# A transformer layer on one core: experts by sorted rows, placed between two attention heads

## The chip, the cores and the metric

The kernel runs on one core of a Trainium2 chip. Five engines work side by side and meet at semaphores: TensorE (PE in the profile, with its weight loads as PEld), VectorE (DVE), ScalarE (ACT), GpSimd (POOL) and SyncE (SP), which here only issues DMAs. ACT and POOL can issue DMAs too. The metric is the device time of one execution in microseconds; the number quoted is the median of three runs. One further execution was profiled, and all rows come from it.

## What is computed

The input x is 2 x 2048 rows of 256 numbers. Every row is normalised, and two branches read it: attention with 16 heads of width 16, and a gated expert layer in which each row uses only the expert with the largest of 8 logits. The experts' result goes through SiLU and multiplies the attention's.

```python
def experts(xf):                                   # xf: 4096 x 256
    logits = einsum('th,eh->te', xf, gate_w)       # 8 experts
    onehot = one_hot(argmax(logits, -1), 8)
    g = einsum('th,ehd->etd', xf, wg)              # wg, wu: 8 x 256 x 64
    u = einsum('th,ehd->etd', xf, wu)
    inter = square(relu(g)) * u * onehot.T[:, :, None]
    return einsum('etd,edh->th', inter, wd)        # wd: 8 x 64 x 256

xn = layernorm(x)
out = x + attention(xn, w_qkv, w_out) * silu(experts(xn))
```

Attention is softmax(q k / 4) v per head, with a rotation (RoPE) on q and k, and an output projection.

## The kernel before, in words

The 4096 rows are 32 tiles of 128. The kernel has three parts.

**The group part.** Eight groups of four tiles. For each tile PE multiplies the transposed rows by the weights of q, k, v and the gate (L757, L758). ACT copies the three results out of PSUM (L376 to L378), DVE rotates q and k (`rotate`, L494 to L501), PE transposes the rotated q and k (L790), ACT copies them as a high part (L385), DVE makes the low part that rounding lost (L528), and SP stores both with four DMAs to `parts_d` in DRAM (L265). Between these steps the group goes through all eight experts densely: `g` and `u` for four pairs of experts (L775, L781), a mask that PE makes of the one-hot choice (L798), DVE's and ACT's work on it (L522, L388, L537), the product with `wd` (L811), and SiLU into `gate` (L393). POOL normalises the next group's rows (L670, L676). PE transposes them (L729).

When the 16 tiles of batch 0 are stored, SP loads the q and k of head 0 back, stacked for two uses (`stack_loads`, L246 to L250): once for the row maxima ("a", partitions 64 up), once for the scores. From group 4 on, the maxima of head 0 are computed beside the group work (L742 on PE, L544 on DVE).

**The heads.** 32 heads (16 per batch), two per turn of a loop of 16 pairs. A head has 16 steps. In a step PE computes four blocks of scores (L838), four blocks for the maxima of a tile 21 steps ahead (L829), and the weighted values (L849); ACT takes the exponentials (L420); DVE reduces the maxima (L582). POOL copies a head's v into place before the head begins (L696, `stage`). SP loads later heads' q and k and stores sums.

**The end.** The output projection (L908), the product with `gate`, the sum with x, and the stores.

The order on each engine is written out by hand, each engine's program is a sequence of its own, and a wait is for a semaphore's count. The lines below are those of the functions that the change touches.

## Time and profile before

| what | us |
|---|---|
| median of 3 runs | 1772.77 (1771.05 to 1774.16) |
| the profiled execution | 1771.24 |
| its span, first to last instruction | 1769.4 |
| PE, DVE, ACT, POOL busy in the span | 1649.1, 1425.9, 1188.7, 56.9 |

The execution has 1.8 us around its span. A step in time is read by the number at the start of a row of the timeline, which is microseconds from the span's start. A group of instructions has the time for which they were busy, and behind it the time the engine stood idle ahead of them with what ended that.

### The profile page before, as it was taken

The page shows a single profiled execution, that of the slowest core. Times are in us where ns is not written, and L with a number is a line of the kernel's source. Part 1 is how long each engine was busy: PE and PEld are TensorE (multiplying, and loading weights), DVE is VectorE, ACT ScalarE, POOL GpSimd, SP SyncE. Part 2 cuts the span into 40 slices and gives each one's busy share as a digit, 9 for nine tenths or more (in the row PEclk, how much of TensorE's full clock was granted, in tenths as well). Part 3 has the DMA queues.
Part 4 walks back from the last instruction along what each step waited for, and adds up shares of the span by engine and source line. Part 5 has one row for each costly group of instructions (what it writes and reads, how often), then busy time and mean ns, then how long its engine had stood idle before and what let it go on. Part 6 is the DMA issues. An engine that isn't in the chain of part 4 may idle for free.

```text
span 1769.4 us, 30282 instructions
## 1 busy us (share of the span) xinstructions
PE 1649.1 (93%) x9536; PEld 717.0 (41%) x9536; DVE 1425.9 (81%) x1541; ACT 1188.7 (67%) x2314; POOL 56.9 (3%) x55
## 2 busy tenths in 40 slices
PE   5999999969999999999999999999999999999998
PEld 2555555433333333333333333333333333333335
DVE  6554666649999999999999999999999999999905
ACT  2333332228788777787777788777877778877781
POOL 1000000000000000000000100000010000000100
PEclk9999999969999999999999999999999999999999
DMA  4222211111111111211111113111111121111203
GB/s 159 65 66 67 77 48 48 49 60 30 43 42 42 42 39 39 70 56 39 39 39 40 43 43 90 44 45 43 42 41 42 61 69 41 39 39 39 58 4 111
DMA packets 71378, 92.66 MB, mean 52 GB/s; under 512 B 20273, under 2 KB 61361, under 8 KB 64177
## 3 DMA queue, kind: packets, MB, share of 16 engines
q1 hardware_dynamic: 65984, 85.23, 15.8%
q10 hardware_dynamic: 5360, 7.03, 1.1%
q8 instruction: 17, 0.28, 0.1%
q14 instruction: 17, 0.13, 0.0%
HBM read 66.01 MB, written 25.43 MB: 52 GB/s over the span
## 4 chain that ended last, share of the span: by engine, by line
PE 74%; ACT 16%; DVE 3%; issue 3%; DMA 3%; SPq 0%; DVEq 0%; ACTq 0%
PE ps L849 29%; PE ps L838 28%; ACT arena L420 16%; PE ps L781 3%; PE ps L811 3%; PE ps L757 3%; PE ps L775 2%; PE ps L758 1%; PE ps L829 1%; PE ps L742 1%; DMA x_sb<-in_x 1%; DVE arena L544 1%; PE ps L790 1%; DMA ks<-parts_d 1%; PE ps L908 1%
## 5 line engine op out<-in xcount | busy, mean ns | idle before, releaser
L582 DVE TENSOR_REDUCE arena<-ps 128x1 f32<-128x1024 f32 x992 | 1174.2, 1219 | 137.0 <-PE ps L829 131.3
L420 ACT ACTIVATE arena<-ps 128x512 f32<-128x512 f32 x2048 | 1059.8, 604 | 263.3 <-PE ps L838 261.8
L838 PE MATMUL ps<-qs,ks 50*128 50x512 f32 x2048 | 746.6, 444 | 62.0 <-ACT arena L420 30.3
L829 PE MATMUL ps<-ks,qs 48*128 48x512 f32 x1984 | 789.3, 470 | 12.8 <-DMA ks<-parts_d 11.8
L838 PEld LDWEIGHTS ps<-qs,ks 50*128 50x128 f32 x2048 | 338.3, 184 | 679.8 <-issue 429.1
L849 PE MATMUL ps<-arena 128*32 128x512 f32 x4096 | 546.2, 605 | 0.8 <-ACT arena L420 0.8
L829 PEld LDWEIGHTS ps<-ks,qs 48*128 48x128 f32 x1984 | 328.7, 185 | 55.1 <-DVE arena L582 13.5
L849 PEld LDWEIGHTS ps<-arena 128*32 128x32 f32 x4096 | 80.6, 108 | 128.8 <-ACT arena L420 114.3
L494 DVE TENSOR_TENSOR arena<-arena,rope 128x512 f32<-128x512 f32 x32 | 28.4, 887 | 86.6 <-ACT arena L378 85.7
L388 ACT ACTIVATE arena<-arena 128x512 f32<-128x512 f32 x32 | 20.1, 629 | 89.7 <-DVE arena L522 89.7
L757 PE MATMUL ps<-arena 128*128 128x512 f32 x128 | 69.4, 625 | 8.0 <-ACT arena L378 7.3
L811 PE MATMUL ps<-arena 128*128 128x256 f32 x256 | 60.7, 398 | 12.3 <-DVE arena L537 12.3
L775 PE MATMUL ps<-arena 128*128 128x512 f32 x128 | 62.6, 612 | 0.0
L781 PE MATMUL ps<-arena 128*128 128x512 f32 x128 | 60.2, 593 | 0.0
L811 PEld LDWEIGHTS ps<-arena 128*128 128x128 f32 x256 | 50.3, 199 | 21.4 <-DVE arena L537 8.1
L696 POOL COPY arena<-v_sb 128x256 f32 x32 | 13.2, 414 | 1267.2 <-ACT arena L412 1266.9
L614 DVE RECIPROCAL arena<-arena 128x16 f32<-128x16 f32 x33 | 8.0, 243 | 55.4 <-DMA arena<-arena 55.4
L376 ACT COPY arena<-ps 128x512 f32<-128x512 f32 x32 | 18.8, 587 | 48.1 <-PE ps L758 48.1
L544 DVE TENSOR_REDUCE arena<-ps 128x1 f32<-128x1024 f32 x32 | 39.1, 1221 | 3.6 <-PE ps L742 3.6
L758 PE MATMUL ps<-arena 128*128 128x264 f32 x128 | 40.4, 398 | 0.0
L758 PEld LDWEIGHTS ps<-arena 128*128 128x128 f32 x128 | 25.4, 198 | 32.9 <-issue 32.9
L393 ACT ACTIVATE gate<-ps 128x512 f32 (+1 forms) x16 | 9.6, 597 | 41.0 <-PE ps L811 40.9
(64 smaller groups left out, 571.0 us busy)
## 6 DMA issues: line engine op xcount, KB each, us to landing
parts_d<-arena SPq DMA_DIRECT2D x128, 128.0 KB, 2.0
qs<-parts_d SPq DMA_DIRECT2D x64, 256.0 KB
ks<-parts_d SPq DMA_DIRECT2D x64, 256.0 KB
qs<-parts_d SPq DMA_DIRECT2D x64, 128.0 KB
ks<-parts_d SPq DMA_DIRECT2D x64, 128.0 KB
onum_d<-arena SPq DMA_DIRECT2D x128, 32.0 KB, 1.9
out<-arena ACTq DMA_DIRECT2D x16, 256.0 KB, 2.4
arena<-onum_d SPq DMA_DIRECT2D x3, 1024.0 KB
```

The source lines that it names most:

```text
L420: nc.scalar.activation(prob[kb % 2][:, c * W:(c + 1) * W], ps[:, bank, :], ACT.Exp, scale=SCALE).then_inc(exp_done[bank], 1)
L494: nc.vector.tensor_tensor(ra.rearrange("p (h d) -> p h d", d=hd), q2, tab[:, :, 0:hd].to_broadcast([P, 2 * QK // DH, hd]), ALU.mult)
L544: nc.vector.tensor_reduce(most[0][:, t, u:u + 1], ps[:, 6:8, :], AX.XY, ALU.max).then_inc(a_reduced[u], 1)
L582: nc.vector.tensor_reduce(most[head_slot][:, tile, u:u + 1], ps[:, AB + 2 * u:AB + 2 + 2 * u, :], AX.XY, ALU.max).then_inc(a_reduced[u], 1)
L757: nc.tensor.matmul(ps[:, o, :], xt, w_sb[:, k, 0:QK], start=(k == 0), stop=(k == KC - 1))
L758: last = nc.tensor.matmul(ps[:, o + 1, 0:VG], xt, w_sb[:, k, QK:QK + VG], start=(k == 0), stop=(k == KC - 1))
L775: last = nc.tensor.matmul(ps[:, o, :], wg_sb[:, k, c * P:(c + 1) * P], xnT[s][:, k, :], start=(k == 0), stop=(k == KC - 1))
L781: last = nc.tensor.matmul(ps[:, o + 1, :], wu_sb[:, k, c * P:(c + 1) * P], xnT[s][:, k, :], start=(k == 0), stop=(k == KC - 1))
L811: last = nc.tensor.matmul(ps[:, 6 + j // 2, (j % 2) * D:(j % 2 + 1) * D], inter[:, c, j * P:(j + 1) * P], wd_sb[:, c, :], start=(c == 0), ...
L829: ins = nc.tensor.matmul(ps[:, AB + c, :], qs[head_slot][ABASE:ABASE + KR, tile * P:(tile + 1) * P].bitcast(F32R), ks[head_slot][ABASE:ABA ...
L838: nc.tensor.matmul(ps[:, bank, :], ks[s][0:KS, kb * P:(kb + 1) * P].bitcast(F32R), qs[s][0:KS, c * W:(c + 1) * W].bitcast(F32R), start=Tru ...
L849: last = nc.tensor.matmul(ps[32 * c:32 * (c + 1), PVB, :], vst[s][:, kb, :], prob[kb % 2][:, c * W:(c + 1) * W], start=(kb == 0), stop=(kb ...
```

## The change

The dense experts leave the group part. In their place:

- **Group part.** The four-tile groups become a stream of tiles: PE makes q, k, v and logits of tile t, and transposes q and k of tile t - 2. The normalised rows go into `gate`, which is free until the experts write it. ACT first issues 13 DMAs that zero a sorted copy of the rows in DRAM (`xs_d`). From tile 20 (`EARLY`) on the maxima of head 0 run beside it, as before from group 4 on. When batch 0 is stored, SP now loads the stacks of heads 0 and 1 together.
- **Routing.** After the last tile DVE finds each row's expert, POOL counts rows per expert by a running sum, PE adds the counts over partitions, and DVE turns them into offsets. Each expert's rows are padded to whole tiles of 128, at most 39 tiles in all (`NF`). DVE also writes the expert of each of the 39 tiles.
- **Scatter and gather.** POOL writes the 4096 rows to their sorted places with 32 indirect DMAs of 128 rows (`place`, while heads 0 and 1 run), and collects the results with 32 more (`collect`, from head 4 on).
- **The experts' stage.** After two pairs of heads (`FB`), all engines leave the heads and go through 39 tiles. The expert's number is read from SBUF into a register of PE, and the weights are addressed by it.

```diff
-                for c in range(EC):
-                    for k in range(KC):
-                        last = nc.tensor.matmul(ps[:, o, :], wg_sb[:, k, c * P:(c + 1) * P], xnT[s][:, k, :],
+                for i in range(NF + 2):
+                    if i < NF:
+                        which[i] = pe.value_load(expert[0:1, i:i + 1], min_val=0, max_val=E - 1)
+                        pe.wait_ge(xs_out, i + 1)
+                        if i:
+                            pe.wait_ge(relu_done, i)
+                            pe.wait_ge(hu_ready, i)
+                        for k in range(KC):
+                            last = nc.tensor.matmul(ps[:, AB + 1, 0:2 * DE], xsT[i % 2][:, k, :],
+                                                    wgu[:, k, bass.ds(which[i], 1), :], start=(k == 0), stop=(k == KC - 1))
+                        last.then_inc(hid_done, 1)
+                    if i + 1 < NF:
+                        turn_sorted(i + 1)
+                    if 1 <= i <= NF:
+                        pe.wait_ge(inter_ready, i)
+                        if i >= 2:
+                            pe.wait_ge(inter_out, i - 1)
+                        nc.tensor.transpose(ps[:, AB + 2, 0:P], inter[(i - 1) % 2], ident[:]).then_inc(inter_turned, 1)
+                    if i >= 2:
+                        pe.wait_ge(inter_out, i - 1)
+                        if i >= 3:
+                            pe.wait_ge(y_out, i - 2)
+                        nc.tensor.matmul(ps[:, AB + 3, 0:D], interT[(i - 2) % 2], wd2[:, bass.ds(which.pop(i - 2), 1), :],
+                                         start=True, stop=True).then_inc(y_done, 1)
...
-            with pe.Fori(0, NP - 1) as pi:
+            with pe.Fori(0, FB) as pi:
+                pair(pi, False)
+            experts()
+            with pe.Fori(FB, NP - 1) as pi:
                 pair(pi, False)
...
+            def load_sorted(i):
+
+                if i >= XR:
+                    sp.wait_ge(xs_turned, i - XR + 1)
+                sp.dma_start(xs[i % XR], xs_d[i * P:(i + 1) * P, :]).then_inc(xs_loaded[i % XR], 16)
...
+            def experts():
+
+                for i in range(NF + 2):
+                    if i + 2 < NF and i + 2 >= XR:
+                        load_sorted(i + 2)
+                    if i >= 2:
+                        store_sorted(i - 2)
...
                 if b == 0:
+                    for i in range(2):
+                        sp.wait_ge(parts_stored[i], PSTORES * NB2)
                     sp.wait_ge(first_ones, 2)
                     stack_loads(sp, 0, qs[0], ks[0], ABASE, a_loaded[0])
                     stack_loads(sp, 0, qs[0], ks[0], 0, loaded[0])
-            sp.wait_ge(u_done, NT)
+                    stack_loads(sp, 1, qs[1], ks[1], ABASE, a_loaded[1])
+                    stack_loads(sp, 1, qs[1], ks[1], 0, loaded[1])
...
+                for t in range(NT):
+                    nc.gpsimd.indirect_dma_start(xs_d, bass.IndirectOffsetOnAxis(ap=pos[:, t:t + 1], axis=0),
+                                                 gate[:, t, :], None).then_inc(rows_sorted, 16)
```

`turn_sorted` waits for a tile's load (four buffers, `XR`), and transposes its two halves. In the stage ACT copies the transposed rows, takes the relu of g and the SiLU of y; DVE forms relu(g) * u * relu(g) and copies its transpose. `store_sorted` waits for the SiLU (`y_out`) and stores the tile.

**On PE, in the group part.** Before, in a group's second half (L757 and L758 are the fourth tile's last products, L775 and L781 the dense experts', L790 transposes, L798 masks):

```order
L757 MATMUL ps<-arena 128x512
L758 MATMUL ps<-arena 128x264
L771 REGISTER_ALU
L775 MATMUL ps<-arena 128x512 x2
L790 MATMUL ps<-ident,arena 128x128 x4
L781 MATMUL ps<-arena 128x512 x2
L794 REGISTER_ALU
L798 MATMUL ps<-ident_b,arena 64x128 x8
```

After, one tile from tile 20 on (L935 and L936 are q, k, v and logits, L958 the early maxima, L921 the next rows' transposes, L946 those of q and k):

```order
L935 MATMUL ps<-arena 128x512
L936 MATMUL ps<-arena 128x264
L958 MATMUL ps<-ks,qs 128x512 x2
L921 MATMUL ps<-ident,gate 128x128 x4
L946 MATMUL ps<-ident,arena 128x128 x4
L958 MATMUL ps<-ks,qs 128x512 x2
```

The experts' products and masks are gone from between the tiles, and the transposes of a tile's q and k come after the products of the tile two later.

**On SP, between the stores of batch 0 and of batch 1.** Before, the eight loads of head 0's two stacks:

```order
L265 DMA parts_d<-arena 128x2x128 x64
L246 DMA qs<-parts_d 32x1x2048
L248 DMA qs<-parts_d 16x2048
L249 DMA ks<-parts_d 32x1x2048
L250 DMA ks<-parts_d 16x2048
L246 DMA qs<-parts_d 32x1x2048
L248 DMA qs<-parts_d 16x2048
L249 DMA ks<-parts_d 32x1x2048
L250 DMA ks<-parts_d 16x2048
L265 DMA parts_d<-arena 128x2x128 x64
```

After, the end of the sixteen, ahead of the stores of batch 1 (L289 to L293 are the same four loads):

```order
L289 DMA qs<-parts_d 32x1x2048
L291 DMA qs<-parts_d 16x2048
L292 DMA ks<-parts_d 32x1x2048
L293 DMA ks<-parts_d 16x2048
L308 DMA parts_d<-arena 128x2x128 x64
```

Eight loads more stand on this queue ahead of the stores of tile 16 and up.

**On PE, between the second and the third pair of heads.** Before there is only the loop's turn. After, one tile of the stage (L1054 turns the rows of the next tile, L1068 reads the expert's number into a register, L1074 is g and u, L1083 turns the product, L1088 is y of the tile two back):

```order
L1068 TENSOR_LOAD arena
L1068 ISA x2
L1074 ISA
L1074 MATMUL ps<-arena 128x128
L1074 ISA
L1074 MATMUL ps<-arena 128x128
L1054 MATMUL ps<-ident,arena 128x128 x2
L1083 MATMUL ps<-ident,arena 128x128
L1088 ISA
L1088 MATMUL ps<-arena 128x256
```

39 such pieces stand between head 3 and head 4, with no work of the heads among them.

## Rows read from the trace of the kernel before

**Rows 1.** Page, part 2: PE's busy share in tenths, 40 slices.

```profile
PE   5999999969999999999999999999999999999998
```

**Rows 2.** Windows: busy us (and instructions) of PE, PEld, DVE, ACT, POOL; clock; DMA.

```profile
80.00:120.00 40.00, 38.73 (x166) 22.18 (x164) 21.75 (x38) 13.75 (x29) 4.17 (x2) 1.00 0.20 53
...
520.00:560.00 40.00, 38.12 (x248) 15.07 (x245) 36.55 (x36) 31.60 (x61) 0.41 (x1) 1.00 0.12 39
```

**Rows 3.** Timeline of PE over one group: start, duration, engine, line, shapes.

```profile
103.68 1.02 PE L757 MATMUL ps<-arena 128*128 128x512 f32 x2
...
114.13 1.88 PE L775 MATMUL ps<-arena 128*128 128x512 f32 x4
...
132.43 1.09 PE L729 MATMUL ps<-ident,arena 128*128 128x128 f32 x8
...
134.79 7.17 PE L811 MATMUL ps<-arena 128*128 128x256 f32 x32 [1.27 <-DVE arena L537]
...
141.80 1.02 PE L757 MATMUL ps<-arena 128*128 128x512 f32 x2
```

**Rows 4.** Timeline: ACT's first copies after the products of a tile.

```profile
31.14 0.58 ACT L376 COPY arena<-ps 128x512 f32<-128x512 f32 x1
...
31.88 0.19 ACT L378 COPY arena<-ps 128x8 f32<-128x8 f32 x1
```

**Rows 5.** Timeline: DVE's rotation of one tile, the low part behind it.

```profile
122.56 0.68 DVE L494 TENSOR_TENSOR arena<-arena,rope 128x512 f32<-128x512 f32 x1
...
124.56 0.68 DVE L528 TENSOR_TENSOR arena<-ps,arena 128x512 fp32r<-128x512 f32 x1
125.16 0.68 DVE L522 TENSOR_TENSOR arena<-arena,ps 128x512 f32<-128x512 f32 x1
```

**Rows 6.** Timeline: the same rotation while POOL normalises rows.

```profile
111.46 2.28 POOL L670 TENSOR_TENSOR arena<-x_sb,mean 128x1024 f32 x1 [34.52 <-DVE arena L501]
...
111.91 2.12 DVE L496 TENSOR_TENSOR arena<-arena,rope 128x256 f32<-128x256 f32 x1
...
113.94 2.13 DVE L498 TENSOR_TENSOR arena<-arena,rope 128x256 f32<-128x256 f32 x1
```

**Rows 7.** Groups by line, 0 to 375 us: busy, mean ns, idle before, releaser.

```profile
L544 DVE TENSOR_REDUCE arena<-ps 128x1 f32<-128x1024 f32 x32 | 39.1, 1221 | 3.6 <-PE ps L742 3.6
...
L377 ACT COPY v_sb<-ps 128x256 f32 (+1 forms) x32 | 12.2, 380 | 0.0
```

**Rows 8.** Timeline of the SP queue: 16 stores, then loads of stacks, and PE.

```profile
120.59 13.23 SPq L265 DMA_DIRECT2D parts_d<-arena  x16
...
355.81 0.65 SPq L246 DMA_DIRECT2D qs<-parts_d  x1
...
362.91 5.46 SPq L248 DMA_DIRECT2D qs<-parts_d  x1
...
369.08 4.70 SPq L250 DMA_DIRECT2D ks<-parts_d  x1
372.92 1.35 PEld L829 LDWEIGHTS ps<-ks,qs 48*128 48x128 f32 x4 [12.15 <-DMA ks<-parts_d]
```

**Rows 9.** Windows while stacks load: the last two numbers are DMA share and GB/s.

```profile
190.00:192.00 2.00, 2.00 (x6) 0.68 (x4) 1.97 (x3) 1.21 (x4) 0.95 (x1) 1.00 0.13 53
```

**Rows 10.** DMA issues: queue, count, KB each, median us from issue to landing.

```profile
parts_d<-arena SPq DMA_DIRECT2D x128, 128.0 KB, 2.0
...
ident<-in_ident ACTq DMA_DIRECT2D x1, 64.0 KB, 3.0
```

**Rows 11.** Timeline: maxima ahead of head 0, and the first exponentials.

```profile
376.71 2.36 DVE L582 TENSOR_REDUCE arena<-ps 128x1 f32<-128x1024 f32 x2 [0.18 <-PE ps L829]
...
379.24 2.36 DVE L582 TENSOR_REDUCE arena<-ps 128x1 f32<-128x1024 f32 x2 [0.18 <-PE ps L829]
...
386.81 3.60 ACT L420 ACTIVATE arena<-ps 128x512 f32<-128x512 f32 x7
```

**Rows 12.** Windows ahead of head 0: the number behind the brackets is the granted clock.

```profile
378.00:380.00 2.00, 2.00 (x4) 0.97 (x4) 1.82 (x2) 0.00 (x0) 0.00 (x0) 0.50 0.13 53
```

More of the change, by code:

```diff
@@ L334, in pair @@
                         load_a(n + 3, 1 - s)
+                    if between and s:
+                        between()
                     store_sums(n, s, pi)
@@ L426, in _ @@
             exps(0, 1, False)
-            with act.Fori(1, NP) as pi:
+            for pi in range(1, FB):
+                for s in range(2):
+                    exps(pi, s, False)
+            experts()
+            with act.Fori(FB, NP) as pi:
                 for s in range(2):
@@ L577, in _ @@
+            for t in range(NT - LAG, NT):
+                low_part(t)
             nc.vector.memset(spread[1], 1.0)
@@ L604, in _ @@
+            choose()
+            for t in range(NT - EARLY, KB):
+                for u in range(2):
+                    reduce(t, 0, t, u)
+            base[0], count[0] = SETUP_STEPS + NT, 0
             for k in range(CUTS):
@@ L679, in group, with step @@
-            def group(n, s, has_next):
-                if has_next:
-                    pool.wait_ge(rope_done, past(n * GT + 1))
-                    center(n + 1, 1 - s)
-                    scale(n + 1, 1 - s)
-            with pool.Fori(0, NG // 2 - 1) as gp:
-                for s in range(2):
-                    group(gp * 2 + s, s, True)
-            group(NG - 2, 0, True)
-            group(NG - 1, 1, False)
+            def step(ins):
+                done[0] += 1
+                ins.then_inc(pool_step, 1)
+                pool.wait_ge(pool_step, done[0])
@@ L817, in _ @@
[L817 to L822 removed]
+            turn_x(0, 0)
+            turn_x(0, 1)
+            for t in range(NT):
+                n, j = divmod(t, GT)
+                qkv(t)
+                if t >= EARLY:
+                    score_early(t - EARLY, 0)
+                if j < 2 and n + 1 < NG:
+                    turn_x(n + 1, j)
+                if t >= LAG:
+                    turn_q(t - LAG)
+                if t >= EARLY:
+                    score_early(t - EARLY, 1)
@@ L824, in score_a @@
+            for t in range(NT - LAG, NT):
+                turn_q(t)
             def score_a(t, head_slot, tile, c):
```

624 lines of the change are left out of this document (373 added, 251 removed).

## The prediction, made before the result was known

> **What bounds the kernel now.** I read the slices first: PE is at nine tenths nearly throughout [rows 1]. Then two windows of 40 us. In the group part PE works 38.7 of 40 us while DVE has 21.8; in the heads PE has 38.1 and DVE 36.6 [rows 2]. So PE sets both, the group part alone has other engines with room, and nothing can be hidden under the heads if it needs PE. The timeline of a group says what PE does in 38.1 us (103.68 to 141.80): 10.4 us of q, k, v and logits, 18.3 us in which the dense experts alternate with the transposes of q and k, 2.4 us of row transposes and a wait, 7.0 us of the products with wd [rows 3]. All but some 13 us of it is the experts'. The first exponential of head 0 stands at 386.8 us [rows 11]; from there to the end the change leaves the program as it is, but for a stage put between heads 3 and 4. The sum is therefore: how much earlier head 0 begins, less what the stage takes.
>
> **Group part, tiles 0 to 19.** A tile's products are 10.4 / 4 = 2.6 us of PE. With the experts gone, what is late next? I follow the loop: products of tile t 2.6, ACT's three copies 0.9 (31.14 to 32.07) [rows 4], DVE's rotation 2.0 and the low part of tile t - 2 0.6 [rows 5], four transposes on PE 0.55 (half of eight in 1.09 [rows 3]), and then the products of tile t + 2, which stand behind these in PE's order. That is 6.7 us, with five hand-offs of 0.1 us 7.2 us, for two tiles: 3.6 each. DVE alone would take 2.6, SP's four stores 13.23 / 4 = 3.3 [rows 8]. POOL's two normalising operations per group make two operations of DVE last 2.1 us in place of 0.4: 3.4 us per four tiles [rows 6]. Fully on the path this makes 4.45, fully absorbed 3.6; I take 4.2, near the upper end, since DVE has only 1 us of slack a tile. ACT's 13 zeroing DMAs stand ahead of its first copy, about 0.45 us each, some 6 us; the experts' weights are no longer loaded beside x, which gives back about 5 us. I leave the first copy at 31.1 us (28 to 37). The low part of tile 15 is ready 17 tiles later: 31.1 + 17 x 4.2 + 3.5 = 106.
>
> **The sixteen loads.** Here I expect the largest loss. A load of 256 KB with an outer dimension of two keeps two of sixteen DMA engines busy (share 0.13) and moves 53 GB/s [rows 9]: 4.9 us. Sixteen loads hold eight of them: 39.6 us on the same two engines. SP itself is held up: in the trace the tenth load of a series waits 5.5 us for room and the twelfth 4.7 us [rows 8]. The stores of tile 16 stand behind, on the same queue and partly the same engines. ACT waits for their landing before it copies the high part of tile 18, and PE, DVE and ACT stop one after the other. From the ready tile 15: stores 3.3, landing 2.0 [rows 10], loads 39.6, stores landing about 3: 48 us, so work goes on at 154. Undisturbed it would have been there at about 119, so the stall is 35 us. Its lower bound is the wait for the first stack alone, which took 17 us from issue in the trace (355.81 to 372.92 [rows 8]): 106 + 5 + 17 = 128, a stall of 9. Its upper bound adds a quarter to the loads: 45.
>
> **Tiles 20 to 31.** DVE now has 2 x 1.22 of maxima [rows 7] with 2.6: 5.1 us, and a hand-off through PE: 5.3. From 154: 2 for what is left of tile 20, 11 x 5.3 = 58, 4 for POOL's last group, 4 for the last two tiles' transposes: 222.
>
> **Up to head 0.** DVE's routing comes first, seven operations, about 2.5 us. Then the maxima of tiles 12 to 20 of the count, nine at 2.53 us (376.71 to 379.24 [rows 11]), 22.8 us, where the kernel before has five left. The counts and PE's first scores are 4 more, and 2 for DVE's twelve operations on the offsets, which stand ahead of the heads' reduces: 253. Before: 386.8. POOL's running sum, about ten small operations, lies under the 22.8 us; without that cover it would cost 5 us. **Gain 134 us**, between 115 (longer tiles and stall) and 160 (short stall).
>
> **The stage.** Nothing of it is in the trace, so I bound a tile from both sides. Below: g and u four passes of 128 columns, 0.43 plus 0.17 to drain, relu 0.2, the copy of the next rows 0.38 [rows 7], hand-offs: 1.5 us. The loop through memory is longer: SP stores tile i - 2 only when its SiLU is done, and issues the load of a later tile behind that store. Turning the loaded rows 0.27, the product's transpose 0.14, y 0.6, SiLU 0.38, store and load issue 0.8, landing 2.0 to 3.0 [rows 10], hand-offs 0.4: 4.6 to 5.6 us for two tiles, 2.3 to 2.8 each. The register load stands between the tiles on PE with no row of its own; it is bounded by 0.1 and by a DMA's way to memory, 2.0 [rows 10]. In the middle it hides in the loop above. If all is in series at half clock, 2.4 us of PE and 2.0 of load: 4.4. I take 2.5: 39 x 2.5 = 98. Entry is 3 us, two last rounds 3, the way back 6 (a table load of ACT, refilling of PE's pipeline, a slow clock): **cost 110 us**, between 70 and 184.
>
> The Trainium skill's "Runtime: NRT & Kernel Launch", section "Instruction fetch mechanics", gives about 0.2 us for a register's load, from HBM, and 1.3 us for several; no run here shows one from SBUF. By 1.3 us the stage stays at 110.
>
> **POOL.** 32 scatters must be issued between the start of head 0 plus 8 us and the start of head 2, since the staging of v for heads 2 and 3 stands behind them; a head is 16 steps of 2.6 us, so 84 - 8 = 76 us, or 2.4 us each. The gathers have 82 us before head 6. The nearest rows are SP's and ACT's issues, 0.35 to 0.85 us, and POOL's own operation of 2.3 us [rows 6, 8]. I take 1.5 us, hidden, cost nothing. If the cover is gone, each us beyond 2.4 costs 32 us, and again in the gathers.
>
> **Sum:** 1771.2 - 134 + 110 = **1747 us** for the profiled execution; the runs' median lies 1.5 us above it, less than I can tell.
>
> **Rivals.**
> 1. *The stage crawls: slower than before.* The break-even is a tile of (134 - 12) / 39 = 3.1 us. The place is PE's order: the register load waits until y is issued, and the next g and u wait for the load. 
> 2. *The loads do not block, and the stage flows.* Stall 10 us, tile 2.2: gain 159, cost 98: 1710. For it: the group part of before did not visibly stop at its eight loads. Against: it had 17 us between them and the next store. Chance 0.2.
> 3. *POOL is late.* An indirect DMA of 3.3 us: 29 us ahead of head 2 and about 24 ahead of head 6: 1800. Nothing in the trace excludes it. Chance 0.1.
> 4. *The change does not do what it says:* the group part stays as long since DVE and SP, not PE, set it. By 3.6 to 4.45 us a tile against 9.5 before this is excluded for the first 20 tiles; it survives only as the stall, which is in the sum.
>
> **How the numbers follow.** My forecast has 0.52, and its own range is 1715 to 1772 (gain 120 to 150, cost 90 to 125, not both at their worst). The whole range leaves out 0.1 at either end: 1695 to 1805. A measurement of this kernel can tell about 0.2%, 3.5 us, from no change. Faster than 1769: rival 2 and nearly all of the forecast's range, 0.70. Within: 0.06. Slower: rivals 1 and 3, less their lower ends, 0.24.
>
> **What would show it.** Head 0's first exponential near 253 us (rival 2: 228). The high part of tile 18 idle ahead for some 35 us, released by a landing of `parts_d`. Tiles 3.6 to 4.45 us apart before, 5.3 after. In the stage, starts of g and u 2.5 us apart (3.6 in rival 1, the wait ending at the register load or at PE), and granted clock. PE's wait for v's staging at heads 2 and 6 zero (rival 3: tens of us). Heads otherwise at 2.6 us a step. I am wrong if the scatter slows the heads' own steps, or if the code, now written out in place of loops, makes engines wait for instructions: nothing here prices either.

## The result

| | before | after |
|---|---|---|
| median, us | 1773.47 (1771.05 to 1774.26, 4 runs) | 1848.97 (1842.84 to 1860.97, 4 runs) |
| span of the profiled execution | 1769.4 | 1848.8 |
| first exponential of head 0 | 386.8 [rows 11] | 282.9 |
| from there to the end | 1382.6 | 1565.9 |

The ratio after to before is 1.0443, 95% interval 1.0418 to 1.0468: 4.4% slower, outside the forecast range. Below, "the rest" is the time from head 0's first exponential to the end of the span. The group part gave back 103.9 us (134 were forecast), and the rest grew by 183.3 us (110 were forecast).

The slices first: page of after, part 2, PE and POOL, 46.2 us each, against [rows 1].

```profile
PE   4763875899877499999999999999999999999998
...
POOL 1120106000002400000000100000001000000100
```

PE now has three holes. The fourth slice is the stacks' loads. The seventh (scatter) and the fourteenth (gather) are where POOL has 6 and 4 tenths of its own. The stage, mostly in the eleventh to thirteenth, has 8, 7 and 7 tenths.

ACT copies a head's sums once (L519, `sums_out`). Two such copies are one head apart, which gives a ruler for the second part. Timeline of ACT in after: start and duration of these copies.

```profile
364.37 0.59 ACT L519 COPY arena<-ps 128x512 f32<-128x512 f32 x1 [0.15 <-PE ps L1004]
406.50 0.59 ACT L519 COPY arena<-ps 128x512 f32<-128x512 f32 x1 [0.18 <-PE ps L1004]
448.33 0.59 ACT L519 COPY arena<-ps 128x512 f32<-128x512 f32 x1
583.89 0.60 ACT L519 COPY arena<-ps 128x512 f32<-128x512 f32 x1
665.88 0.59 ACT L519 COPY arena<-ps 128x512 f32<-128x512 f32 x1 [0.23 <-PE ps L1004]
```

A head without disturbance takes 42 us (364.37 to 406.50, 406.50 to 448.33). Head 0, with the scatter, takes 81.5 us from its first exponential. Head 4, with the gather, takes 82.0 (583.89 to 665.88). What happens in head 4 is in the timeline of all engines: the number in brackets is the idle time ahead of the instruction.

```profile
599.27 0.95 POOL L867 DMA_INDIRECT gate<-ys_d,arena  x1 [0.30 <-issue]
...
602.02 0.60 ACT L527 ACTIVATE arena<-ps 128x512 f32<-128x512 f32 x1 [2.91 <-issue]
602.66 0.28 PEld L993 LDWEIGHTS ps<-qs,ks 50*128 50x128 f32 x1 [2.41 <-issue]
602.66 0.79 PE L993 MATMUL ps<-qs,ks 50*128 50x512 f32 x1 [1.69 <-issue]
...
623.10 0.95 POOL L867 DMA_INDIRECT gate<-ys_d,arena  x1 [0.30 <-issue]
623.72 0.60 ACT L527 ACTIVATE arena<-ps 128x512 f32<-128x512 f32 x1 [21.11 <-remote]
...
624.37 0.79 PE L993 MATMUL ps<-qs,ks 50*128 50x512 f32 x1 [18.88 <-issue]
...
629.32 1.23 DVE L642 TENSOR_REDUCE arena<-ps 128x1 f32<-128x1024 f32 x1 [24.68 <-remote]
```

POOL issues one gather every 1.25 us, from 585 to 625 us. From 604.7 to 623.7 no other engine does anything but finish one product. The profile names no releaser for these waits: "issue" is none that it shows, "remote" is a semaphore event whose source it does not know. The program has none of the three wait for POOL there, except for v, which was staged before the first gather. Counted one to one, product by product, the exponential at 623.72 reads the scores that PE finished at 603.45 (602.66 + 0.79), 20 us earlier. So what is late is the hand-off from one engine to the next, not an engine's own work; how it comes to be late the profile does not show. The windows show the same, against 38.12 of 40 us before [rows 2] (busy us and instructions of PE, PEld, DVE, ACT, POOL; granted clock; DMA share; GB/s):

```profile
280.00:320.00 40.00, 21.67 (x92) 8.15 (x91) 17.23 (x26) 13.64 (x25) 27.24 (x32) 0.63 0.24 87
480.00:560.00 80.00, 60.40 (x340) 38.67 (x336) 30.65 (x103) 37.52 (x105) 0.00 (x0) 0.98 0.34 103
600.00:640.00 40.00, 15.40 (x51) 5.19 (x53) 8.54 (x8) 6.92 (x14) 19.21 (x21) 0.50 0.26 77
```

The DMA engines are at a quarter in these windows (at 0.37 in 605 to 623 us alone), so they are not what is full. TensorE's granted clock falls to 0.50, its 1.2 GHz, in the hole. In the stage it is 0.98.

The group part, in the order of time (timelines of ACT's queue, ACT and PE):

```profile
26.77 11.22 ACTq L478 DMA_DIRECT2D xs_d<-arena  x13
38.03 0.59 ACT L461 COPY arena<-ps 128x512 f32<-128x512 f32 x1 [11.04 <-PE ps L936]
...
96.64 0.66 PE L921 MATMUL ps<-ident,gate 128*128 128x128 f32 x4 [3.93 <-POOL gate L827]
...
123.22 0.68 DVE L617 TENSOR_TENSOR arena<-ps,arena 128x512 fp32r<-128x512 f32 x1
...
144.19 1.22 PE L958 MATMUL ps<-ks,qs 48*128 48x512 f32 x2 [13.42 <-DMA ks<-parts_d]
...
178.79 0.59 ACT L469 CAST arena<-ps 128x512 fp32r<-128x512 f32 x1 [31.72 <-DMA parts_d<-arena]
```

The thirteen zeroing DMAs keep ACT from its first copy for 11.2 us, 0.86 us each. PE waits at the first tile of a group for the rows that POOL normalises. The low part of tile 15 is made at 123.2. The first stack makes PE wait 13.4 us ahead of the first maxima (L958). The sixteen loads stop ACT for 31.7 us ahead of the high part of tile 18, released by a landing of `parts_d`, as the forecast had it.

### The profile page after: what moved, and what is told of

Its sections match the earlier page's. It is cut to its first block, busy times and chain, and to the rows that moved or that the text cites. A ratio compares the mean times of both kernels' runs of the same rounds, so it can differ in the third digit from the quotient of the medians.

```text
span 1848.8 us, 29654 instructions
## 1 busy us (share of the span) xinstructions
PE 1598.4 (86%) x9121; PEld 681.0 (37%) x9121; DVE 1395.5 (75%) x1573; ACT 1191.3 (64%) x2361; POOL 128.9 (7%) x142
## 4 chain that ended last, share of the span: by engine, by line
PE 63%; ACT 17%; DMA 5%; issue 5%; DVE 4%; another core or an unknown queue 3%; SPq 2%; POOL 1%; ACTq 1%; DVEq 0%; POOLq 0%
PE ps L1004 27%; PE ps L993 27%; ACT arena L527 15%; DMA arena<-xs_d 3%; PE ps L935 2%; PE ps L984 2%; PE ps L936 1%; DVE arena L642 1%; DMA x_sb<-in_x 1%; DMA parts_d<-arena 1%; PE ps L1118 1%; PE ps L958 1%; PE ps L1074 1%; PE ps L1088 1%
## 5 line engine op out<-in xcount | busy, mean ns | idle before, releaser
L993 PE MATMUL ps<-qs,ks 50*128 50x512 f32 x2048 | 767.8, 453 | 110.9 <-ACT arena L527 45.7
L984 PE MATMUL ps<-ks,qs 48*128 48x512 f32 x2000 | 816.3, 480 | 11.7 <-issue 6.3
L874 POOL COPY arena<-v_sb 128x256 f32 (+1 forms) x32 | 13.9, 436 | 1337.6 <-ACT arena L519 1298.3
L935 PE MATMUL ps<-arena 128*128 128x512 f32 x128 | 83.6, 741 | 0.7 <-ACT arena L452 0.7
L461 ACT COPY arena<-ps 128x512 f32<-128x512 f32 x32 | 18.8, 589 | 96.7 <-PE ps L936 96.7
L946 PE MATMUL ps<-ident,arena 128*128 128x128 f32 x128 | 23.2, 311 | 33.4 <-DVE arena L617 33.4
L921 PE MATMUL ps<-ident,gate 128*128 128x128 f32 x64 | 13.1, 340 | 42.4 <-POOL gate L827 25.2
L469 ACT CAST arena<-ps 128x512 fp32r<-128x512 f32 x32 | 19.0, 593 | 44.2 <-DMA parts_d<-arena 32.4
L617 DVE TENSOR_TENSOR arena<-ps,arena 128x512 fp32r<-128x512 f32 x32 | 21.9, 683 | 33.4 <-ACT arena L469 33.4
L936 PE MATMUL ps<-arena 128*128 128x264 f32 x128 | 45.1, 438 | 0.0
L936 PEld LDWEIGHTS ps<-arena 128*128 128x128 f32 x128 | 29.1, 227 | 41.0 <-issue 41.0
L1074 PE MATMUL ps<-arena 128*128 x156 | 28.8, 310 | 9.5 <-issue 7.7
```

The costliest lines, as they stand in the source:

```text
L617: nc.vector.tensor_tensor(lo, ps[:, 5, :].rearrange("p (m t) -> p m t", m=HM), pst[t % 2][:, 0:HM, :], ALU.subtract).then_inc(pt_out, 1)
L935: nc.tensor.matmul(ps[:, o, :], xt, w_sb[:, k, 0:QK], start=(k == 0), stop=(k == KC - 1))
L936: last = nc.tensor.matmul(ps[:, o + 1, 0:VG], xt, w_sb[:, k, QK:QK + VG], start=(k == 0), stop=(k == KC - 1))
L946: last = nc.tensor.transpose(ps[:, 5, q * P:(q + 1) * P], rq[t % 2][:, q * P:(q + 1) * P], ident[:])
L984: ins = nc.tensor.matmul(ps[:, AB + c, :], qs[head_slot][ABASE:ABASE + KR, tile * P:(tile + 1) * P].bitcast(F32R), ks[head_slot][ABASE:ABA ...
L993: nc.tensor.matmul(ps[:, bank, :], ks[s][0:KS, kb * P:(kb + 1) * P].bitcast(F32R), qs[s][0:KS, c * W:(c + 1) * W].bitcast(F32R), start=Tru ...
```

## The experiments

Thirteen kernels and the kernel after. Their main numbers, all in us: the time of the run, head 0's first exponential, the rest, head 0 (with the scatter), and the heads in which the gathers are issued.

| kernel | time | first exp. | rest | head 0 | gather's heads |
|---|---|---|---|---|---|
| after | 1848.97 | 282.9 | 1565.9 | 81.5 | 82.0 |
| e1_later_turn | 1852.48 | 281.9 | 1569.0 | 79.9 | 84.9 |
| e2_one_per_step | 1776.06 | 276.9 | 1497.2 | 44.3 | 45.1 + 47.6 |
| e3_plain_dmas | 1765.93 | 276.9 | 1487.3 | 44.5 | 46.4 |
| e4_no_indirect | 1770.21 | 279.5 | 1489.0 | 44.1 | none: 44.9, 43.0 |
| e5_bursts | 1813.59 | 277.6 | 1533.9 | 45.4 | 55.2 + 59.7 + 53.3 |
| e6_plain_pool | 1771.59 | 280.1 | 1489.8 | 44.3 | 43.4 |
| e7_quarter_bytes | 1851.16 | 285.8 | 1563.6 | 78.8 | 80.8 |
| g1_spread_loads | 1746.74 | 250.4 | 1494.3 | 47.2 | 43.6 + 46.2 |
| g2_table_once | 1732.67 | 250.4 | 1480.2 | 44.6 | 44.6 + 44.0 |
| h2_fixed_expert | 1733.12 | 249.8 | 1481.2 | 44.1 | 46.5 + 49.0 |
| g3_group_part | 1724.94 | 237.1 | 1485.8 | 44.3 | 44.6 + 47.5 |
| g4_gather_slower | 1716.75 | 235.8 | 1480.7 | 44.5 | 43.6, 43.1, 41.9, 42.4 |
| n1_own_pause | 1737.65 | 249.8 | 1486.1 | 44.5 | 46.5 + 47.2 |

All but after and g4 are single executions, and the four of after lie up to 18 us apart. The first exponential of kernels with the same group part differs by up to 6 us from one to the next, so the parts are compared, not the totals.

### Is it the indirect DMAs, and what about them?

**e4_no_indirect.** Both loops of `indirect_dma_start` are left out.

```diff
-                for t in range(NT):
-                    nc.gpsimd.indirect_dma_start(xs_d, bass.IndirectOffsetOnAxis(ap=pos[:, t:t + 1], axis=0),
-                                                 gate[:, t, :], None).then_inc(rows_sorted, 16)
...
-                for t in range(NT):
-                    nc.gpsimd.indirect_dma_start(gate[:, t, :], None, ys_d,
-                                                 bass.IndirectOffsetOnAxis(ap=pos[:, t:t + 1], axis=0)).then_inc(gate_ready, 16)
```

> Neither scatter nor gather is issued: the experts work on the zeroed copy, and the product at the end takes the normalised rows in place of the experts' result. The rest of the program is that of after. Theories A and B: the time of a head returns to that of before (first head 42 to 45 us instead of 82) and the kernel takes 1849 - 37.5 - 52 = 1760 us, plus or minus 6. Theory C (code): the holes stay, 1849.

The sums' copies, timeline of ACT:

```profile
323.63 0.59 ACT L519 COPY arena<-ps 128x512 f32<-128x512 f32 x1 [0.15 <-PE ps L997]
...
541.27 0.60 ACT L519 COPY arena<-ps 128x512 f32<-128x512 f32 x1
586.21 0.59 ACT L519 COPY arena<-ps 128x512 f32<-128x512 f32 x1 [0.23 <-PE ps L997]
```

Head 0 takes 44.1 us and head 4 takes 44.9: the scatter costs 37.3 us and the gather 37.1. The rest is 1489.0 against 1565.9, so the indirect DMAs cost **76.9 us**. I had put 52 us on the gather in the expectation, by reading one long idle as a loss; the ruler of copies says 37, and the kernel came at 1770.21, above the 1760 plus or minus 6 that I expected. The rest is still 106.4 us above that of before: this is the stage, with the table loads behind it (g2 below).

**e1_later_turn.** The gathers are issued after v is staged for heads 6 and 7, in the second turn of the loop.

```diff
-            collect()
             for s in range(2):
                 stage(0, FB + 1, s, FB + 1)
+            collect()
```

> The same kernel as after, but the 32 gathers are issued one pair of heads later, in the second turn of the loop that follows the stage; everything is still computed. In the kernel after, head 4 and 5 lose about 52 us while POOL issues the gathers, and PE's long idle is put down to 'issue'. Theory A (each indirect DMA that POOL prepares holds up the hand-offs of the other engines while it is prepared): the hole of some 50 us moves to heads 6 and 7, the time stays at 1849 us, plus or minus 8. Theory B (the hole comes from moving the 4 MB): the same as A, 1849. Theory C (the engines run out of code, since the gathers fall into the first turn of a loop, whose code isn't there yet): no hole at heads 6 and 7 and none at heads 4 and 5, about 1797 us.

Timeline of ACT:

```profile
668.82 0.61 ACT L519 COPY arena<-ps 128x512 f32<-128x512 f32 x1
715.75 2.08 ACT L527 ACTIVATE arena<-ps 128x512 f32<-128x512 f32 x4 [20.42 <-remote]
753.74 0.59 ACT L519 COPY arena<-ps 128x512 f32<-128x512 f32 x1 [0.23 <-PE ps L1004]
```

The hole moves with the gathers: the head from 668.82 takes 84.9 us, and ACT stands for 20.4. The theory of missing code, which "issue" suggested, has fallen.

**e7_quarter_bytes.** Rows of 64 numbers to and from an array of their own, zeroed by four more DMAs.

```diff
-                    nc.gpsimd.indirect_dma_start(xs_d, bass.IndirectOffsetOnAxis(ap=pos[:, t:t + 1], axis=0),
-                                                 gate[:, t, :], None).then_inc(rows_sorted, 16)
+                    nc.gpsimd.indirect_dma_start(few_d, bass.IndirectOffsetOnAxis(ap=pos[:, t:t + 1], axis=0),
+                                                 gate[:, t, 0:64], None).then_inc(rows_sorted, 16)
```

> The 32 scatters and 32 gathers are indirect as in the kernel after and follow on each other without a pause, but each row has 64 numbers (256 bytes) and goes to and comes from an array of its own, so a quarter of the bytes moves and the experts work on the zeroed copy. Four more zeroing DMAs stand in ACT's queue at the start, some 3 us. Theory A/A2 (the preparing, which goes by the number of rows): pitch 1.27 us and the same two losses, 38 and 52 us, plus or minus 10: 1850. Theory B (the moving of bytes): losses of a quarter, some 22 us together, 1783.

Waits of the whole kernel, us in total, times, longest:

```profile
ACT arena L531 <- remote: 66.0, 12, 22.5
DVE arena L646 <- remote: 64.2, 5, 20.5
```

Heads of 78.8 and 80.8 us with a quarter of the bytes. Moving the data is not the cause.

**e3_plain_dmas** and **e6_plain_pool.** In e3 the scatters are 32 plain DMAs of POOL, the gathers 32 plain ones of SP. In e6 both are 64 plain DMAs of half a tile, issued by POOL.

```diff
+                    nc.gpsimd.dma_start(xs_d[t * P:(t + 1) * P, :], gate[:, t, :]).then_inc(rows_sorted, 16)
...
+                sp.dma_start(gate[:, t, :], ys_d[t * P:(t + 1) * P, :]).then_inc(gate_ready, 16)
```

```diff
+                    for h in range(2):
+                        nc.gpsimd.dma_start(xs_d[t * P:(t + 1) * P, h * P:(h + 1) * P],
+                                            gate[:, t, h * P:(h + 1) * P]).then_inc(rows_sorted, 16)
```

> The rows are not sorted here, so the experts work on the wrong rows, with the same number of tiles and bytes: the 32 scatters become 32 plain DMAs of 128 KB issued by POOL, and the 32 gathers become 32 plain DMAs of 128 KB issued by SP after the stage. Theory A (preparing on POOL): the gather's 52 us are gone, since POOL prepares nothing there; the scatter's 37 us shrink if a plain DMA is prepared faster than 1.27 us, and stay if not: 1760 to 1797 us. Theory B (moving 4 MB in rows of 1 KB beside the heads): both losses stay, 1849. Theory C: both stay, 1849.

> The rows are not sorted and not collected by index, so the experts work on the wrong rows; tiles and bytes are the same. In place of 32 indirect DMAs POOL issues 64 plain DMAs of half a tile (128 rows of 512 bytes) in each of the two places, without a pause; at the 0.54 us each that the run with 32 plain ones shows, this is 34 us of uninterrupted issue, nearly the 40 us of the indirect ones. Theory P (any DMA that POOL prepares does it, and the 17 us of the earlier run were too short for it to build up): a standstill in both places, 20 to 50 us each, 1800 to 1850. Theory I (only the indirect form does it): no standstill, 1760 to 1770 us.

POOL's timeline in e6:

```profile
284.93 34.08 POOL L859 DMA_DIRECT2D xs_d<-gate  x64 [0.72 <-POOL arena L854]
...
544.70 34.31 POOL L869 DMA_DIRECT2D gate<-ys_d  x64 [0.19 <-issue]
```

POOL issues without a pause for 34 us, 0.53 us each, and heads 0 and 4 take 44.3 and 43.4 us: no loss. The same bytes, by plain DMAs of 128 rows each, disturb nobody. It is the indirect form, or what only it does here, which is to go to scattered rows: an indirect DMA to rows that lie in order was not run, so the two are not told apart. e3 agrees for the scatter (44.5); its gather's head took 46.4, 1.5 us more than in e4.

### How often may they be issued?

**e2_one_per_step.** POOL waits for one step of the heads before each.

```diff
                 for t in range(NT):
+                    pool.wait_ge(a_scored[1], AHEAD + 1 + t)
                     nc.gpsimd.indirect_dma_start(xs_d, bass.IndirectOffsetOnAxis(ap=pos[:, t:t + 1], axis=0),
                                                  gate[:, t, :], None).then_inc(rows_sorted, 16)
+                    if t == KB + 4:
+                        stage(0, 1, 0, 1)
```

> Everything is computed, but POOL waits for a step of the heads before each of the 32 scatters and each of the 32 gathers, so that one is issued every 2.6 us in place of every 1.27 us. Theory A with a fixed price for each indirect DMA (1.2 us in the scatter, 1.6 us in the gather): the loss is spread but stays, 1849 us plus or minus 10. Theory A2 (what holds up the others is that POOL issues them without a pause, the delay builds up over some 8 to 20 us and then everything stands): with a pause behind each, nearly all of the 90 us come back, 1760 to 1775 us. Theory B (data): 4 MB over twice the time, at most half of the loss stays, 1800. Theory C (code): nothing changes, 1849.

The rest falls from 1565.9 to 1497.2, 8.2 above the kernel without any: 69 of the 77 us come back with the same 64 DMAs. The theory of a fixed price per DMA has fallen. The kernel's 1776.06 is 1 us above the range expected of the theory that holds.

**e5_bursts.** Bursts of 4 per 4 steps in the scatter, of 8 per 8 steps in the gather.

```diff
+                    if t % 4 == 0:
+                        pool.wait_ge(a_scored[1], AHEAD + 4 + t)
...
+                    if t % 8 == 0:
+                        pool.wait_ge(a_scored[1], FB * 2 * KB + AHEAD + 8 + t)
```

> Everything is computed. The scatters are issued in bursts of 4, one burst every 4 steps of the heads, and the gathers in bursts of 8, one burst every 8 steps; within a burst nothing is waited for. A burst of 4 is about 5 us of POOL, one of 8 about 10 us. In the kernel after, the first idle time of the other engines comes some 5 to 12 us behind the first DMA, the standstill 11 to 19 us behind it. Theory A2 (the delay builds up while they are issued without a pause, and is gone with a pause): bursts of 4 cost under 3 us over both heads together, bursts of 8 cost between 0 and 15 us; the whole kernel 1770 to 1790 us. Theory A (a price per DMA, which the spacing of the run with one per step hid for another reason): each burst stops the others for its length, 1849.

The first burst of 8 (timelines of POOL, ACT and DVE):

```profile
571.63 1.01 POOL L873 DMA_INDIRECT gate<-ys_d,arena  x1 [24.10 <-PE ps L990]
...
580.46 0.95 POOL L873 DMA_INDIRECT gate<-ys_d,arena  x1 [0.30 <-issue]
...
580.29 1.09 ACT L527 ACTIVATE arena<-ps 128x512 f32<-128x512 f32 x2 [3.39 <-remote]
...
582.41 2.36 DVE L642 TENSOR_REDUCE arena<-ps 128x1 f32<-128x1024 f32 x2 [4.95 <-remote]
```

The bursts of 4 cost 1.3, 3.0 and 1.6 us in three heads, 6 together. The bursts of 8 cost 10.3, 16.6 and 11.3, 38 together: as much as 32 without a pause. My expectation was wrong in all three numbers: at most 15 us for the bursts of 8, under 3 us for those of 4, and 1770 to 1790 us for the kernel. The first idle time comes after the fourth or fifth DMA, 5 to 6 us after the first of the burst.

**n1_own_pause.** On g2 (below), without waits for steps: POOL clears a small array twice behind each scatter and once behind each gather.

```diff
-                    pool.wait_ge(a_scored[1], AHEAD + 1 + t)
                     nc.gpsimd.indirect_dma_start(xs_d, bass.IndirectOffsetOnAxis(ap=pos[:, t:t + 1], axis=0),
                                                  gate[:, t, :], None).then_inc(rows_sorted, 16)
+                    for _ in range(2):
+                        step(nc.gpsimd.memset(held[0], 0.0))
```

> The run with the table loaded once, but POOL waits for no step of the heads: behind each scatter it clears a small unused array twice, behind each gather once, each clearing about 0.45 us and waited for, so that the pitch is about 2.2 us in the scatter and 1.75 us in the gather, against 1.27 in the kernel after and 2.6 with one per step. Everything is computed. Theory D (what counts is the share of POOL's time that goes to preparing indirect DMAs; the other engines' hand-offs are late only while that share is nearly one, or builds up when it is over some bound): nearly no loss in the scatter (first head 44 to 46 us), less than half of the 37 us loss in the gather; the kernel 1733 to 1755 us. Rival E (it was the meeting with the heads' steps that helped, which keeps each DMA away from the hand-offs): both losses back in full, about 37 us each, 1805 us. Rival F (POOL being busy without a pause, with whatever work): both losses back or larger.

POOL's timeline in the gather:

```profile
515.37 0.96 POOL L875 DMA_INDIRECT gate<-ys_d,arena  x1 [0.27 <-POOL arena L877]
516.32 0.44 POOL L877 MEMSET arena<- 128x384 f32 x1
517.03 0.95 POOL L875 DMA_INDIRECT gate<-ys_d,arena  x1 [0.27 <-POOL arena L877]
```

POOL is as busy as ever, and the holes are gone. At a pitch of 2.15 us head 0 takes 44.5 us (0.4 lost), at 1.66 us the gather's two heads 93.7 us against 88.0 in e4 (5.7 lost), at 1.25 one head loses 37. So 0.4 us more between two indirect DMAs takes most of the loss away, whoever makes the pause. The gathers that are paced by steps, 2.6 us apart, lose 0.5 to 7.5 us in their two heads (e2, g1, g2, h2, g3), so these single runs do not tell 1.66 from 2.6 us.

### The group part, the stage, and the loop behind it

**g1_spread_loads.** On e2: after batch 0 only the first four loads, the other twelve one per tile.

```diff
                     stack_loads(sp, 0, qs[0], ks[0], ABASE, a_loaded[0])
-                    stack_loads(sp, 0, qs[0], ks[0], 0, loaded[0])
-                    stack_loads(sp, 1, qs[1], ks[1], ABASE, a_loaded[1])
-                    stack_loads(sp, 1, qs[1], ks[1], 0, loaded[1])
...
+                    if b and 2 <= t < 14:
+                        head, base, done = ((1, ABASE, a_loaded[1]), (0, 0, loaded[0]), (1, 0, loaded[1]))[(t - 2) // 4]
+                        stack_loads(sp, head, qs[head], ks[head], base, done, ((t - 2) % 4,))
```

> The run with one indirect DMA per step, with one edit in the group part: after batch 0 only the four loads of head 0's first stack are issued, and the other twelve follow one at a time behind the stores of tiles 18 to 29. Everything is computed. My theory of the stall (sixteen loads hold two DMA engines for some 40 us and the stores behind them wait): the stall of 30 us ahead of the high part of tile 18 shrinks to under 12 us, the first exponential comes at 277 - 22 = 255 us and the kernel takes 1754 us, plus or minus 8. Rival (the loads only delay what DVE and PE would be late with anyway, or each single load holds up the stores of its tile by 5 us): first exponential 270 to 277, kernel 1769 to 1776.

Timeline of PE:

```profile
140.75 1.22 PE L966 MATMUL ps<-ks,qs 48*128 48x512 f32 x2 [11.18 <-DMA ks<-parts_d]
```

The stall of 31.7 us is gone; what stays is the wait for the first stack, 11.2 us (13.4 in after). The first exponential comes at 250.4, 26.5 us earlier.

**g2_table_once.** While comparing e4 with before I found that a pair of heads takes 85.0 us behind the stage and 84.2 before. The cause is in e4's timeline of ACT and DVE, once per turn of the loop:

```profile
1136.43 1.28 ACT L527 ACT_TABLE_LOAD   x1
...
1139.43 1.23 DVE L642 TENSOR_REDUCE arena<-ps 128x1 f32<-128x1024 f32 x1 [0.94 <-PE ps L977]
```

and in the groups of after and of g2 (busy us, mean ns):

```profile
L527 ACT ACT_TABLE_LOAD x15 | 19.2, 1283 | 1.2 <-PE ps L993 0.9
```

```profile
L531 ACT ACT_TABLE_LOAD x2 | 2.6, 1283 | 0.9 <-PE ps L1003 0.9
```

The loop is entered with SiLU's table, so the exponential's load stands inside it and runs in each of 14 turns. The Trainium skill's "ScalarE: Activation LUTs", section "What ACT_TABLE_LOAD costs", gives about 1283 ns for a load; the trace agrees, 1283 ns. g2 writes the first pair behind the stage out:

```diff
+            for s in range(2):
+                exps(FB, s, False)
-            with act.Fori(FB, NP) as pi:
+            with act.Fori(FB + 1, NP) as pi:
```

> The run with spread loads, with one edit: ACT's exponentials of heads 4 and 5 are written out ahead of its loop, so that the loop is entered with the exponential's table in place. In the kernel after, ACT's L527 has 15 table loads of 1.28 us, one at the entry and one in each of the loop's 14 turns, and a pair of heads takes 85.0 us there against 84.2 before. Theory (the load stands inside the loop because SiLU was the table ahead of it, and 0.8 of its 1.28 us are not hidden): 2 loads are left (one ahead of head 0, one ahead of head 4), a pair takes 84.2 us again, the kernel 1746.7 - 11 = 1736 us, plus or minus 3. Rival (the 0.8 us are the loop's turn or its code): loads gone, time 1745 to 1748.

A pair takes 84.2 us again (1021.75 to 1105.97), and the rest is 14.1 us shorter than in g1. From the end of head 5 on the two kernels differ by 9.9 us: these are the loads of the 13 turns behind it, 0.76 us each. The other 4.2 lie before, mostly in heads 0 and 5, whose length differs by 2 to 3 us among runs with the same pacing; with them the kernel came out just below the expected 1733 to 1739.

**h2_fixed_expert.** On g2; the experts' numbers are constants, so no register is read.

```diff
-                        which[i] = pe.value_load(expert[0:1, i:i + 1], min_val=0, max_val=E - 1)
+                        which[i] = i % E
```

> The run with the table loaded once, but the expert of a tile is a constant and no register is read on PE, so the rows go through the wrong experts; everything else is the same. Theory (the stage's loop is the one through memory and the queue, the register's load hides beside it): the stage's 39 tiles take the same time within 5 us, kernel 1731 to 1737. Rival (the load stands in series on PE): 39 times 0.6 to 1.0 us come back, kernel 1697 to 1713.

The copies around the stage, first in h2, then in g2 (timelines of ACT):

```profile
377.85 0.58 ACT L523 COPY arena<-ps 128x512 f32<-128x512 f32 x1 [0.15 <-PE ps L1014]
...
507.15 0.61 ACT L523 COPY arena<-ps 128x512 f32<-128x512 f32 x1
```

```profile
379.16 0.59 ACT L523 COPY arena<-ps 128x512 f32<-128x512 f32 x1
...
512.22 0.60 ACT L523 COPY arena<-ps 128x512 f32<-128x512 f32 x1
```

129.3 against 133.1 us, 3.8 less. But over the same stretch the kernels whose stage is unchanged lie between 130.9 (e3) and 137.2 us (e2), so one execution of each only bounds the price of the 39 register loads, at 0.2 us each or less. How the price is hidden shows in PE's groups of the stage, first g2, then h2 (idle time behind the second bar):

```profile
L1084 PE MATMUL ps<-arena 128*128 x156 | 28.8, 310 | 9.5 <-issue 7.5 <-ACT arena L499 1.5
L1064 PE MATMUL ps<-ident,arena 128*128 128x128 f32 x78 | 16.9, 300 | 10.4 <-DMA arena<-xs_d 9.6 <-DVE arena L648 0.5
```

```profile
L1084 PE MATMUL ps<-arena 128*128 128x128 f32 x156 | 28.1, 304 | 1.3 <-ACT arena L499 1.3
L1064 PE MATMUL ps<-ident,arena 128*128 128x128 f32 x78 | 17.2, 303 | 19.4 <-DMA arena<-xs_d 18.8 <-DVE arena L648 0.5
```

Without the loads PE's idle time ahead of g and u (L1084) falls from 9.5 to 1.3 us, 0.2 us a tile, and its wait for the rows from memory (L1064) grows from 9.6 to 18.8. The tile stays bound by the loop through memory. The total is the same since the two heads of the gather took 7.0 us more in h2 than in g2, within the spread of this paced gather in the other kernels.

**g3_group_part.** On g2: the zeroing DMAs one per tile from tile 3 on, POOL's normalising two tiles earlier.

```diff
+                if 3 <= t < 3 + NF // ZR:
+                    zero_rows(t - 3)
...
-                    pool.wait_ge(rope_done, (n - 1) * GT)
+                    pool.wait_ge(rope_done, (n - 1) * GT - 2)
```

> The run before with two edits in the group part, seen at different places of the trace: ACT issues the 13 zeroing DMAs one per tile from tile 3 on, not ahead of its first copy, and POOL normalises a group's rows two tiles earlier. Theory: the first copy of a tile comes at 27 to 28 us in place of 38 (11 us), and the tile period falls from 5.0 to 4.2 us since PE no longer waits for POOL at a group's first tile (7 groups, 3 to 5 us each in the first five): first exponential 250 - 11 - 16 = 223 us, kernel 1709 us, plus or minus 8. Rival (POOL's two operations slow DVE wherever they lie, and 0.86 us of issue in each tile is paid there): first exponential 238, kernel 1725.

Timeline of PE in the first tile:

```profile
31.42 1.11 PE L934 MATMUL ps<-ident,gate 128*128 128x128 f32 x4 [9.52 <-POOL gate L836]
```

13.3 us of the 27 expected. ACT's first copy came 11 us earlier, but PE then waited for POOL's first group until 31.4, which the zeroing had covered. The period of a tile fell from 4.97 to 4.42 us (from POOL's second start to its sixth, 16 tiles), not to 4.2. PE's waits for POOL at the later groups, 3.5 to 3.9 us in g2, are gone. So the theory did not hold in full: the recorded rival, that POOL's two operations slow DVE wherever they lie and that the zeroing DMAs' issue is paid in each tile, named 238 us and 1725, and 237.1 and 1724.94 came. Its two parts were not taken apart.

**g4_gather_slower.** On g3: one gather per two steps, with v of the later heads staged in between.

```diff
-                    pool.wait_ge(a_scored[1], FB * 2 * KB + AHEAD + 1 + t)
+                    pool.wait_ge(a_scored[1], FB * 2 * KB + AHEAD + 1 + 2 * t)
```

> The run with both edits of the group part, with the gathers one per two steps of the heads in place of one per step, so over four heads; everything is computed. With one per step the second head of the gather takes 46 to 47.6 us against 43.0 without gathers. Theory (what is left of the loss is still the density of the gathers): heads 5 to 8 at 42.0 to 42.5 us, 3 us less than the run before, so 1706 us if that is 1709; against the kernel before a ratio near 0.963. Rival (the 3 to 4 us come from somewhere else, such as the stage's aftermath): the same as the run before within 1.5 us.

The gather's heads are at 43.6, 43.1, 41.9 and 42.4 us, the rest 5.1 us shorter than in g3. In four runs g4 has 1716.75 us (1714.51 to 1719.49) and a ratio to before of 0.9681, interval 0.9663 to 0.9700. It computes everything and **beats both kernels**: 3.2% faster than before. The 1706 us that I expected came from the 1709 expected of g3, which g3 missed.

## Why the prediction was wrong, step by step

| step | forecast | measured | adds to the time |
|---|---|---|---|
| first copy of ACT | 31.1 | 38.0 | 6.9 |
| low part of tile 15 | 106 | 123.2 | 10.3 more |
| work goes on after the loads | 154 | 178.8 | 7.6 more |
| first exponential | 253 | 282.9 | 5.1 more |
| the stage | 110 | 106.4 | -3.6 |
| indirect DMAs on POOL | 0 | 76.9 | 76.9 |
| sum | | | 103.2 |

The forecast for the span was 1769.4 - 134 + 110 = 1745.4; it was 1848.8, and the table accounts for the 103.4 us between them within rounding.

**The step that failed is "hidden, cost nothing" for POOL's indirect DMAs.** Their duration was bounded well: 1.25 to 1.27 us each against 1.5 assumed and a limit of 2.4, and v was staged in time, so rival 3 did not occur. The kernel did come out slower, as rivals 1 and 3 had it, but for neither's reason. What I did not price is that their issue slows engines that wait for nothing from POOL. I named it at the end ("if the scatter slows the heads' own steps") and gave it no share of the range, since nothing in the trace of before shows an indirect DMA. That reason calls for a wider range: an operation without a row should have had a bound for what it does to others, such as its whole length of issue, 32 x 1.5 = 48 us twice. The 76.9 us lie inside this bound, and with it the range would have reached 1841 us, well past the kernel before.

**The group part** had the right mechanism and sizes too small, 30 us in all; the gain of 103.9 us lies outside the 115 to 160 that the forecast gave it. The zeroing DMAs took 0.86 us each, not 0.45, though rows 8 had issues up to 0.65 and the text itself a span to 0.85. A tile took 5.0 us, not 4.2: POOL normalises a group only when the rotation of the group before is done, and PE turns those rows in the first tile after, so PE waited 3.9 us there (L921), 1 us a tile; I had counted POOL's load on DVE and not this wait. Taking it away in g3 brought 0.55 us of the period and not the whole 1 us, so part of it stands for something else that g3 did not single out. The stall behind the loads was forecast as 48 us from the ready tile 15 to the next work and was 55.6; g1 shows the loads as its cause, since spreading them brought 26.5 us. Rival 2 (no blocking) is thereby refuted; rival 4 (no gain at all) is refuted by the 103.9 us. That the loads hold two DMA engines, as the forecast had it, no run tested by itself.

**The stage** was right within 4 us, in part by luck, since two errors cancel. DVE's product that reads g and u, first and last tile (timeline of DVE in after):

```profile
492.94 0.22 DVE L747 TENSOR_TENSOR arena<-arena,ps 128x64 f32<-128x64 f32 x1 [2.25 <-ACT arena L505]
...
577.53 0.22 DVE L747 TENSOR_TENSOR arena<-arena,ps 128x64 f32<-128x64 f32 x1 [1.00 <-ACT arena L505]
```

These are 38 steps of 2.23 us on average, not 2.5: many near 2.0, and five of 3.0 to 4.7. That is 39 x 0.27 = 10.5 us less, and 10 us more for the table loads in each turn, which I counted once. The register load is hidden beside the loop through memory, as the forecast assumed (h2). The Trainium skill's "Runtime: NRT & Kernel Launch", section "Instruction fetch mechanics", has 0.2 us for a load from HBM, which is near the 0.2 us a tile for which PE stands here, and 1.3 us for several, which does not show here. Rival 1 fell: the granted clock in the stage is 0.98. In 480 to 560 us PE was busy for 60.4 of 80 us and kept its high clock; in the hole of the gather, busy for 15.4 of 40, it was at 0.50. The Trainium skill's "TensorE: Matmul & The Clock Gate", section "HAM oscillation — how this bites in real kernels", had made me give rival 1 its weight; the stage's pauses were not of that kind, the holes were.

Without the 76.9 us the kernel would have been at 1772, the same as before and not 25 us faster: inside the range, but without the gain, since the group part gave back 30 us less than forecast.

## What to carry to other kernels

Issue indirect DMAs with a pause between them, by a wait for some regular event of the main work or by POOL's own work. Here scatters 2.15 us apart cost 0.4 us in all, gathers 2.6 us apart up to 7.5 us, gathers 5.2 us apart nothing that shows (g4), and 1.25 us apart about 1.2 us each. Before entering a loop that uses one activation function, see that its table is in place; here the load was repeated in every turn. When an operation has no row in the trace, bound what it does to the other engines as well as how long it takes, and read losses by a ruler (the same instruction one period later) rather than by the longest idle time.

## What the runs showed of the hardware

- An indirect DMA of 128 rows takes POOL 0.95 us, with 0.30 us to the next, for rows of 1 KB and of 256 bytes alike. A plain one of 64 or 128 KB follows on the last after 0.53 or 0.54 us.
- Indirect DMAs in an unbroken row hold up the hand-offs among PE, ACT and DVE, from the fourth or fifth on in the gather and from about the seventh in the scatter (after 5 to 9 us), up to a standstill of 19 us, although the program has none of them wait for POOL. The profile has "issue" and "remote" there. Plain DMAs issued by POOL for 34 us do not do it. What is full, or held, in the chip meanwhile no run here shows; that stays open. The Trainium skill's "SBUF — State Buffer", section "SBUF: two separate sides", describes a conflict in the other direction, in which DVE's work delays what POOL writes for its DMAs; DVE was idle in the standstill, so that conflict is not this one.
- In the standstill TensorE's granted clock goes down to 0.50, its 1.2 GHz, which makes the steps that still run slower: a product of scores takes 0.50 us at 595.58 and 0.79 us at 602.66.
